# Two transformer layers in one kernel: how the router's choices, rank sums, slot map, compressed keys and last sums are divided among the engines

## What is computed

```
x = h                                        # (4, 256, 256): 1024 tokens of 256
xn = layernorm(x)
x = x + attention0(xn) + moe0(xn)            # moe0: 32 experts, top 6, and 2 shared experts
xn = layernorm(x)
x = x + attention1(xn) + moe1(xn)            # moe1: 8 experts, top 2
```

## Time and profile before

| | us |
|---|---|
| median of 3 runs | 557.43 (556.4 to 557.67) |
| the profiled execution | 554.29 |
| its span in the trace | 552.5 |
| TensorE busy | 511.5 (93%) |
| VectorE busy | 358.2 (65%) |
| ScalarE busy | 312.7 (57%) |
| GpSimd busy | 295.2 (53%) |

### The profile page before, as it was taken

How to read it: one execution, slowest core, us unless ns; L and a number is a source line. 1 busy time by engine, 2 the same in 40 slices (tenths; PEclk the granted TensorE clock), 3 DMA queues, 4 the chain that set the end, 5 groups by cost and what they waited for, 6 DMA issues and landing times.

```text
span 552.5 us, 9828 instructions
## 1 busy us (share of the span) xinstructions
PE 511.5 (93%) x2951; PEld 393.0 (71%) x2951; DVE 358.2 (65%) x1042; ACT 312.7 (57%) x737; POOL 295.2 (53%) x225
## 2 busy tenths in 40 slices
PE   7998999989899999999999999999977989899981
PEld 6556778879678788788788888888755445465561
DVE  6698835728568366566486383433576979997643
ACT  1224266777786676775776765756422358475520
POOL 1002366787678467475676676743130065888860
PEclk9799999999999999999999999999999899999996
DMA  7981457997999767488586697762675022756677
GB/s 241 356 286 41 138 131 162 225 247 191 322 224 274 191 151 175 109 188 182 120 187 147 141 212 153 178 131 30 171 236 183 1 66 58 102 90 99 89 87 229
DMA packets 87395, 90.41 MB, mean 164 GB/s; under 512 B 26768, under 2 KB 75344, under 8 KB 86960
## 3 DMA queue, kind: packets, MB, share of 16 engines
q1 hardware_dynamic: 66720, 61.50, 38.4%
q0 software_dynamic: 19584, 27.24, 28.4%
q10 hardware_dynamic: 1040, 1.05, 0.6%
HBM read 65.32 MB, written 22.60 MB: 159 GB/s over the span
## 4 chain that ended last, share of the span: by engine, by line
PE 63%; DVE 9%; issue 9%; DMA 8%; ACT 6%; POOL 5%; SPq 0%; POOLq 0%; ACTq 0%; DVEq 0%
PE bank L971 12%; PE bank L567 9%; PE bank L980 6%; PE bank L979 6%; DMA expert_sums<-expert_weights,token_of_slot 4%; PE bank L559 4%; PE bank L524 4%; PE bank L492 3%; PE bank L961 3%; POOL tiles L1173 3%; PE bank L576 3%; POOL expert_sums L1180 2%; PE bank L512 2%; PE bank L542 2%; ACT normed L641 2%
## 5 line engine op out<-in xcount | busy, mean ns | idle before, releaser
L941 POOL DMA_INDIRECT expert_sums<-expert_weights,token_of_slot x79 | 128.2, 1623 | 57.3 <-ACT expert_weights L1003 30.6
L933 POOL DMA_INDIRECT expert_weights<-normed_x,token_of_slot x79 | 87.7, 1110 | 110.3 <-DVE token_of_slot L373 49.0
L971 PE MATMUL bank<-expert_weights 128*88 128x128 f32 x632 | 82.6, 273 | 0.4 <-ACT expert_weights L996 0.4
L971 PEld LDWEIGHTS bank<-expert_weights 128*88 128x88 f32 x632 | 72.8, 156 | 1.6 <-issue 1.3
L567 PE MATMUL bank<-out_weights,expert_weights 128*128 128x256 f32 x256 | 59.9, 380 | 2.6 <-DVE residual L830 1.8
L1180 POOL DMA_INDIRECT expert_sums<-expert_weights,token_of_slot x23 | 46.4, 2019 | 13.7 <-issue 5.6
L567 PEld LDWEIGHTS bank<-out_weights,expert_weights 128*128 128x128 f32 x256 | 46.5, 190 | 9.4 <-issue 2.6
L787 DVE SCALAR_TENSOR_TENSOR expert_weights<-bank,blocks_valid 128x64 f32<-128x64 f32 x32 | 7.2, 224 | 63.1 <-ACT expert_weights L655 63.1
L979 PE MATMUL bank<-expert_weights 88*128 88x256 f32 x158 | 47.1, 379 | 0.0
L980 PE MATMUL bank<-expert_weights 89*128 89x256 f32 x158 | 47.1, 379 | 0.0
L1003 ACT ACTIVATE expert_weights<-bank,chosen_bf 128x256 f32<-128x256 f32 x79 | 37.7, 477 | 16.4 <-PE bank L980 16.0
(11 more groups left out here) (283 smaller groups left out, 1071.0 us busy)
## 6 DMA issues: line engine op xcount, KB each, us to landing
expert_weights<-experts_out SPq DMA_DIRECT2D x79, 192.8 KB, 3.5
expert_weights<-experts_in SPq DMA_DIRECT2D x79, 176.0 KB, 3.7
expert_weights<-L_ffn_wi SPq DMA_DIRECT2D x32, 128.0 KB
expert_weights<-w_comp SPq DMA_DIRECT2D x1, 2048.0 KB, 12.1
expert_weights<-fold_g SPq DMA_DIRECT2D x1, 2048.0 KB, 14.5
expert_sums<-zeros SPq DMA_DIRECT2D x2, 1024.0 KB, 13.5
expert_weights<-L_ffn_wo SPq DMA_DIRECT2D x16, 128.0 KB
normed<-expert_sums SPq DMA_DIRECT2D x2, 1024.0 KB, 6.7
```

The source lines that it names most:

```text
L933: nc.gpsimd.indirect_dma_start(xt0[g % 4], None, xn0, bass.IndirectOffsetOnAxis(ap=MAP[:, g:g + 1], axis=0)).then_inc(gathered[g % 4], 16)
L941: nc.gpsimd.indirect_dma_start(sums0[g % 2], bass.IndirectOffsetOnAxis(ap=MAP[:, g:g + 1], axis=0), yt0[g % 4], None, compute_op=ALU.add). ...
L971: ins = nc.tensor.matmul(ps[5][0:DHB, c * P:(c + 1) * P], w[:, k * DH + c * DHB:k * DH + (c + 1) * DHB], xT0[g % NXT][:, k * P:(k + 1) * P ...
```

## The change

Six things are altered. (1) Layer 0's logits come in two banks, 2 and 6, and `lg_ps` is raised after each half; VectorE adds the bias and makes the choices of a half at a time (`choose_dve`). The first `shared_up` moves between the two halves in TensorE's program. (2) The running sum over the tiles is gone from VectorE, in both layers. TensorE makes it: one matmul of all nine groups of columns by the triangular matrix, then eight by the ones, each over all later tiles through a repeated operand. (3) The 79-wide one-hots of the map are made in two steps: GpSimd subtracts (slot tile less column number), and ScalarE squares that and takes relu(token - token * square), which is the token's number where the difference is 0, and 0 elsewhere. VectorE keeps the 128-wide ones. `TOK` has eight more columns, the negated token numbers. (4) The compressed keys of the two halves of the contraction go to rows 0 to 63 and 64 to 127 of bank 2, and VectorE adds the two. (5) The last sums are loaded in quarters, each with a semaphore, and added in quarters. (6) The last `take_project1` goes ahead of these sums.

```
-        TOK = sb("tokens", NT + 1)
+        TOK = sb("tokens", 2 * NT + 1)
...
-        MASKB = sb("chosen_bf16", NT * E0, BF16)
+        MASKB = sb("chosen_bf16", (NT + 1) * E0, BF16)
...
+        def choose_dve(dve, st, E, K, layer, tiles):
             ONEH, PROD, LOGIT, CUM = route_room(layer)
             lg, tp, ti = v3(LOGIT[:, 0:NT * E], NT), v3(TOP[:, :], NT), v3(TOPI[:, :], NT)
-            tf, g3 = v3(TOPF[:, :], NT), v3(GATE[:, 0:NT * K], NT)
+            tf, lo, hi = v3(TOPF[:, :], NT), tiles[0], tiles[-1] + 1
             oh = ONEH[:, 0:NT * K * E].rearrange("p (t k e) -> p t k e", t=NT, k=K)
-            pr = PROD[:, 0:NT * K * E].rearrange("p (t k e) -> p t k e", t=NT, k=K)
-            for t in range(NT):
+            for t in tiles:
                 st(nc.vector.max(tp[:, t, :], lg[:, t, :]))
             st.wait()
-            for t in range(NT):
+            for t in tiles:
                 st(nc.vector.max_index(ti[:, t, :], tp[:, t, :], lg[:, t, :]))
             st.wait()
-            st.link(nc.vector.tensor_copy(TOPF[:, :], TOPI[:, :]))
-            for t in range(NT):
+            st.link(nc.vector.tensor_copy(tf[:, lo:hi, :], ti[:, lo:hi, :]))
+            for t in tiles:
                 st(nc.vector.tensor_tensor(oh[:, t], bc(IOTA[:, 0:E].unsqueeze(1), [P, K, E]),
                                            bc(tf[:, t, 0:K].unsqueeze(2), [P, K, E]), ALU.is_equal))
...
-            st.link(nc.vector.tensor_reduce(v3(CUM[:, 0:NT * E], NT),
-                                            ONEH[:, 0:NT * K * E].rearrange("p (t k e) -> p t e k", t=NT, k=K),
+            st.link(nc.vector.tensor_reduce(v3(CUM[:, 0:NT * E], NT)[:, lo:hi, :],
+                                            ONEH[:, lo * K * E:hi * K * E].rearrange("p (t k e) -> p t e k", t=hi - lo, k=K),
                                             AX, ALU.add))
-            st(nc.vector.tensor_copy(MASKB[:, 0:NT * E], CUM[:, 0:NT * E]))
-            st.link(nc.vector.memset(CUMB[:, 0:E], 0.0))
-            for t in range(1, NT):
-                st.link(nc.vector.tensor_tensor(CUM[:, t * E:(t + 1) * E], CUM[:, (t - 1) * E:t * E],
-                                                CUM[:, t * E:(t + 1) * E], ALU.add))
-            nc.vector.tensor_copy(CUMB[:, E:(NT + 1) * E], CUM[:, 0:NT * E]).then_inc(chosen, 1)
+        def route_dve(dve, st, E, K, layer):
+            CUM, g3, tp = route_room(layer)[3], v3(GATE[:, 0:NT * K], NT), v3(TOP[:, :], NT)
+            st.link(nc.vector.memset(MASKB[:, NT * E:(NT + 1) * E], 0.0))
+            nc.vector.tensor_copy(MASKB[:, 0:NT * E], CUM[:, 0:NT * E]).then_inc(chosen, 1)
...
+        MAPPS, EXPPS, LOGITB = 320, 400, (2, 6)
...
-            st.link(nc.vector.tensor_scalar(MTILE, MTILE, MAGIC, -MAGIC, ALU.add, ALU.add))
+            nc.vector.tensor_scalar(MTILE, MTILE, MAGIC, -MAGIC, ALU.add, ALU.add).then_inc(map_t, 1)
+            dve.wait_ge(map_t, 1)
             st.link(nc.vector.scalar_tensor_tensor(out=v3(MPOS, NT), in0=v3(MTILE, NT), scalar=-float(P), in1=slots, op0=ALU.mult, op1=ALU.add))
         def map_dve(dve, t):
             k = slice(t * K0, (t + 1) * K0)
             if t >= 2:
-                dve.wait_ge(map_c, t - 1)
                 dve.wait_ge(map_ps, t - 1)
-            nc.vector.tensor_tensor(v3(mt[t % 2], K0), bc(IOTA[:, 0:NT0].unsqueeze(1), [P, K0, NT0]),
-                                    bc(MTILE[:, k].unsqueeze(2), [P, K0, NT0]), ALU.is_equal).then_inc(map_b, 1)
             nc.vector.tensor_tensor(v3(ma[t % 2], K0), bc(IOTA[:, :].unsqueeze(1), [P, K0, P]),
                                     bc(MPOS[:, k].unsqueeze(2), [P, K0, P]), ALU.is_equal).then_inc(map_a, 1)
+        def map_pool(pool, t):
+            if t >= 2:
+                pool.wait_ge(map_c, t - 1)
+            nc.gpsimd.tensor_tensor(v3(mt[t % 2], K0), bc(IOTA[:, 0:NT0].unsqueeze(1), [P, K0, NT0]),
+                                    bc(MTILE[:, t * K0:(t + 1) * K0].unsqueeze(2), [P, K0, NT0]), ALU.subtract).then_inc(map_b, 1)
         def map_act(act, t):
             act.wait_ge(map_b, t + 1)
+            nc.scalar.activation(mt[t % 2], mt[t % 2], ACT.Square).then_inc(map_q, 1)
+            act.wait_ge(map_q, t + 1)
             if t >= 2:
                 act.wait_ge(map_ps, t - 1)
-            nc.scalar.activation(mb[t % 2], mt[t % 2], ACT.Copy, scale=TOK[:, t:t + 1]).then_inc(map_c, 1)
+            nc.scalar.activation(mb[t % 2], mt[t % 2], ACT.Relu, scale=TOK[:, NT + 1 + t:NT + 2 + t], bias=TOK[:, t:t + 1]).then_inc(map_c, 1)
...
+            nc.tensor.matmul(bank[:, 0:(NT + 1) * E], BEFOREB[:, :], MASKB[:, 0:(NT + 1) * E], start=True, stop=False)
             for t in range(NT):
-                nc.tensor.matmul(bank[:, t * E:(t + 1) * E], BEFOREB[:, :], MASKB[:, t * E:(t + 1) * E],
-                                 start=True, stop=False)
-                nc.tensor.matmul(bank[:, t * E:(t + 1) * E], ONESB[:, :], CUMB[:, t * E:(t + 1) * E],
-                                 start=False, stop=True)
-            nc.tensor.matmul(bank[:, NT * E:(NT + 1) * E], ONESB[:, :], CUMB[:, NT * E:(NT + 1) * E],
-                             start=True, stop=True).then_inc(rank_ok, 1)
+                later = bank[:, (t + 1) * E:(NT + 1) * E].rearrange("p (n e) -> p n e", e=E)
+                ins = nc.tensor.matmul(later, ONESB[:, :], bc(MASKB[:, t * E:(t + 1) * E].unsqueeze(1), [P, NT - t, E]),
+                                       start=False, stop=(t == NT - 1))
+            ins.then_inc(rank_ok, 1)
...
+            choose_dve(dve, st, E1, K1, 1, range(NT))
             route_dve(dve, st, E1, K1, 1)
...
-            for b in range(B - 1):
+            for b in range(B):
                 take_project1(dve, b)
-            dve.wait_ge(ao_rd, B - 1)
+            dve.wait_ge(ao_rd, B)
             for i in range(2):
                 r = (NT0 + NT1 + i) % 2
-                dve.wait_ge(sum1_ld[r], 16)
-                if i == 0:
-                    st.link(nc.vector.tensor_tensor(X[:, :], X[:, :], SUMS1[r], ALU.add))
-                else:
-                    for b in range(B):
-                        x, y = (z[:, b * TPB * HID:(b + 1) * TPB * HID] for z in (X[:, :], SUMS1[r]))
-                        ins = nc.vector.tensor_tensor(x, x, y, ALU.add)
-                        ins.then_inc(f_ok, 1)
-            dve.wait_ge(f_ok, B)
-            take_project1(dve, B - 1)
+                for b in range(B):
+                    dve.wait_ge(sum1_ld[r][b], 16)
+                    if i:
+                        dve.wait_ge(part_ok, b + 1)
+                    x, y = (z[:, b * TPB * HID:(b + 1) * TPB * HID] for z in (X[:, :], SUMS1[r]))
+                    nc.vector.tensor_tensor(x, x, y, ALU.add).then_inc(f_ok if i else part_ok, 1)
...
-                    sp.dma_start(v3(SUMS1[r], NT), sums1[r][0:T, :].rearrange("(t p) d -> p t d", p=P)).then_inc(sum1_ld[r], 16)
+                    for b in range(B):
+                        sp.dma_start(v3(SUMS1[r], NT)[:, b * TPB:(b + 1) * TPB, :],
+                                     sums1[r][b * S:(b + 1) * S, :].rearrange("(j p) d -> p j d", p=P)).then_inc(sum1_ld[r][b], 16)
                 rows = out.rearrange("b (j p) d -> b p j d", p=P)
                 for b in range(B):
                     sp.wait_ge(f_ok, b + 1)
-                    if b == B - 1:
-                        sp.wait_ge(ao_rd, B)
...
+                pool.wait_ge(ld_c, N_C)
+                pool.wait_ge(map_t, 1)
+                for t in range(NT):
+                    map_pool(pool, t)
                 pool.wait_ge(map_ok, 1)
...
+                st(nc.vector.tensor_scalar(TOK[:, NT + 1:], TOK[:, 0:NT], -1.0, None, ALU.mult))
                 dve.wait_ge(ld_rt, 32)
-                st.link(nc.vector.tensor_tensor(v3(route_room(0)[2], NT), v3(ps[2][:, 0:NT * E0], NT),
-                                                bc(RB[:, :].unsqueeze(1), [P, NT, E0]), ALU.add))
+                for hf in range(2):
+                    lo, hi = hf * NT // 2, (hf + 1) * NT // 2
+                    dve.wait_ge(lg_ps, hf + 1)
+                    st.link(nc.vector.tensor_tensor(v3(route_room(0)[2], NT)[:, lo:hi, :], v3(ps[LOGITB[hf]][:, 0:NT * E0], NT)[:, lo:hi, :],
+                                                    bc(RB[:, :].unsqueeze(1), [P, NT // 2, E0]), ALU.add))
+                    choose_dve(dve, st, E0, K0, 0, range(lo, hi))
                 route_dve(dve, st, E0, K0, 0)
...
-                dve.wait_ge(ck_ps, 1)
+                dve.wait_ge(ck_ps, KC)
                 ckn = CKR[:, 0:D]
-                st.link(nc.vector.tensor_copy(CKR[:, D:], ps[2][0:NB * B, 0:D]))
+                st.link(nc.vector.tensor_copy(CKR[:, 0:D], ps[2][NB * B:2 * NB * B, 0:D]))
+                st.link(nc.vector.tensor_tensor(CKR[:, D:], ps[2][0:NB * B, 0:D], CKR[:, 0:D], ALU.add))
...
-                            ins = nc.tensor.matmul(ps[2][:, t * E0:(t + 1) * E0], xnT3[:, k, t * P:(t + 1) * P],
```

(15 more changed lines are left out.)

25 lines of the change are left out of this document (11 added, 14 removed).

## The result

The changed kernel takes 548.43 us (median of four runs, 546.55 to 551.75) against 556.91 us for the kernel before in the same rounds (555.64 to 557.67). The ratio is 0.986, 95% interval 0.983 to 0.990: 8.5 us less by the medians and 7.6 by the ratio, where 7.9 were forecast and 549.5 us predicted. A repeat gave 0.985.

A forecast was written before the change was run, and what follows sets the result against it. TensorE is busy 93% of the span, but the change touches four stretches where it is not the bound. Terms -5.2 + 3.2 - 1.4 - 2.5 - 2.0 = -7.9 us gave 549.5 us, range 547 to 552 (546.3 to 554.0 with (a), (b), (c)).

The forecast's parts named there:

- choices and ranks, layer 0: Opening: choices in halves, rank sums on TensorE and a clock staying at 1.00 start L304 at 24.9, not 30.07: -5.2 us.
- slot map: Layer 0's map, one-hots partly moved to GpSimd and ScalarE: last `map_pe` 16.3 us after L340, before 13.1: +3.2 us.
- compressed keys: 64 key records in column tiles take 5.0 us, not 7.34; TensorE reaches L1940 at 65.5, not 66.9: -1.4 us.
- middle, 75 to 200 us: Between 75 and 390 us nothing is changed, so a lead won before should pass through: 0.
- layer 1 to its first gather: Layer 1: seven additions and a copy leave VectorE's chain, and TensorE's wait ahead of L1066 shortens: -2.5 us.
- the end: Last sums: VectorE has one quarter left to add after the loads; stores eat part: -2.0 us, between -1.0 and -2.7.
- rival (b): Opening: the clock falls anyway, total -4.6 us, 552.8 us; chance 0.14.
- rival (d): Slot map: GpSimd's subtraction far slower than its memset, deciding from 2.0 us; with 2.5, 561.5 us; chance 0.08.
- rival (a): Slot map: GpSimd and VectorE run freely, map +1.9, total -9.2 us, 548.2 us; chance 0.18.
- the step that charged the map the sum of both engines: Slot map: GpSimd and VectorE block each other, so eight times (1.0 + 0.88) and 0.25 ahead, 15.3 us.
- If the clock holds 2.8, if it falls 1.6: Layer 1: the map ends 2.8 us sooner if TensorE's clock holds, 1.6 if it falls.
- rival (c): Middle full of transfers, or layer 1 gives 1.6 and stores 1.0: about -4.5 us, 552.9 us; chance 0.12.

The follow-up runs named there:

- last quarter late: Changed kernel, but VectorE adds the attention's last quarter behind seven of the eight additions of the expert sums: 547.91 us, ratio 0.983.

## Why the prediction was right, and where it was not

By steps, each against what the traces measured:

| step | forecast | measured |
|---|---|---|
| choices and ranks, layer 0 | -5.2 | -5.1; -6.0 against the second profile of before |
| slot map | +3.2 | +1.8 three times, +2.7 to +3.2 four times |
| compressed keys | -1.4 | -1.4 |
| middle, 75 to 200 us | 0 | +1.6 in nine of twelve executions, 0 in three |
| layer 1 to its first gather | -2.5 | -1.7 to -4.0, -2.9 between the means |
| the end | -2.0 | -0.7 in the mean of seven (-2.2 or +1.4) |
| whole | -7.9 | -8.5 and -8.2 by the medians, -7.6 and -8.6 by the ratios |

**Choices and ranks** came out as worked: the clock held at 1.00, the first half's choices hid in the wait for the second half's logits. The experiments, each taking out one part, divide the term: the halves 1.7 us, the ranks 1.9, and the remaining 1.5 lies ahead of both: the logits end sooner because the clock holds. With the choices whole they still begin at 17.61 us, where before it was 19.18. The clock fell at 14 to 15 us in both profiles of before and held until 26 us in all twelve of changed kernels, which is why rival (b) fell.

**The slot map** came out near its number, but not by the forecast's reason, and that is luck. GpSimd's subtraction takes 0.97 us alone; 1.0 was taken, and rival (d), which needed 2.0, fell. The two engines do hold each other up: no one-hot of VectorE ran in under 1.12 us beside GpSimd where it takes 0.95 alone, so the premise of rival (a) is false. But the step that charged the map the sum of both engines was too dear. Two one-hots took 3.34 us together, 1.67 each beside one subtraction, where the sum of both rows taken alone is 1.93 (1.88 was charged); the blocking is not complete. The Trainium skill, in "SBUF — State Buffer", section "SBUF: two separate sides", has an exclusive lock of the shared port pair for whole instructions, by which a pair could not take less than the sum of the two, 1.93 by these rows; the measured 1.67 decides, so by these rows part of an instruction's span lies outside the lock.

At 1.67 a pair no longer sets the pace alone. Here is the stretch from ScalarE's first Square to its last Relu, first in the run with the end as before, where the clock held, then in the first profile of the changed kernel, where it fell:

```profile
33.52:46.64 13.12, 9.26 (x70) 6.32 (x70) 11.93 (x10) 12.38 (x23) 10.45 (x7) 1.00 0.43 133
```

```profile
33.30:47.52 14.22, 10.74 (x70) 7.56 (x70) 11.09 (x10) 12.41 (x23) 9.42 (x7) 0.88 0.37 115
...
38.62 0.39 ACT L1712 ACTIVATE expert_weights<-bank 128x256 f32<-128x256 f32 x1 [0.88 <-PE bank L1924]
```

ScalarE is busy for 12.4 of 13.1 us: it is the limit, with VectorE and GpSimd close beneath it. In the three executions in which the clock held (choices whole, end as before, last quarter late), the last `map_pe` started 15.0 to 15.1 us after the map's first step, where the prediction worked out 14.9 with ScalarE as the limit and 16.3 with the sum. So the term was +1.8 and not +3.2. Where the clock fell near 35 to 39 us (three executions), ScalarE's take-out of keys and values waited 0.88 to 1.30 us for TensorE, which the forecast had not charged and which made up for the step that was too dear. That ScalarE is the limit is read from the traces; no run changed its work alone. From the map's first step to its end were 13.9 us in all seven kernels with the one-hots on VectorE (before among them), 15.7 in three of seven on GpSimd, and 16.7 to 17.1 in four. The fourth of these is the one with running sums: its clock held in the map but fell just ahead of it (26.5 to 29.9 us), so that ScalarE was held up by the shared experts' relu and began its first Square 3.15 us after the map's first step in place of 1.66.

**Layer 1** showed the clearest quantity of the study. From the copy of the chosen (L283) to the first gather pass, in fourteen executions, only these: 20.30, 21.27 and 21.36 us with running sums (before twice, and the experiment), and with the ranks on TensorE 17.33 or 17.34 six times and 18.64 or 18.65 five times. The 1.66 us of VectorE's additions is in all; the rest is the clock. The chain of the repeat shows the dear case, columns as in the earlier trace rows:

```profile
423.54 5.40 PE bank L1070 x8
428.94 1.87 PE bank L1093 x8
```

In the first profile the same eight records took 3.70 us at a clock of 1.00, VectorE was the limit, and the chain came to

```profile
440.43 0.04 issue
440.48 1.93 PE bank L1093 x7
```

without an idle gap on VectorE. "If the clock holds 2.8, if it falls 1.6" was right both ways; what the prediction didn't see is that the same program does the one or the other from run to run.

**The step that failed** is the sentence that between 75 and 390 us nothing is changed and a lead passes through. From the first to the thirty-third scatter of layer 0 pass 124.05 to 124.63 us in five executions (before twice, the repeat, and two with the map on VectorE) and 125.08 to 128.92, 126.1 in the mean, in nine. The nine are exactly those in which the scatter of the ninth tile held GpSimd for 3.25 to 3.69 us instead of 1.6. The traces show the cause. In the nine the scatter started 0.05 to 0.50 us after the start of VectorE's L782 and ended 1.46 us after its end, every time; in the five it started 0.02 to 1.00 us ahead of L782 and took 1.58. From the ninth scatter to the tenth pass 4.8 to 5.3 us in the nine and 3.5 to 4.5 in the five. It is the blocking that the prediction had read from the earlier trace rows and charged to the map alone: it did not ask where else a scatter stands this close to a VectorE instruction with two inputs in SBUF, and in the profile of before 0.02 us decided it.

The scatter of the twenty-eighth tile was caught by the same instruction in four executions (2.99 to 3.55 us, again ending 1.46 behind it); in two of these the distance to the thirty-third stayed at 124.6, so there it cost nothing. The loss is one that rival (c) allowed for, 1.6 us against the 3.4 by which (c) lies above the forecast, though (c) gave full transfers as the reason; it is nearly all of the lead in one execution. A lead isn't lost everywhere in the middle: from 200 us on, the distance between any two executions stays the same but for single tiles that come back to it (188.2 us from the thirty-third scatter to the last of layer 0 in all fourteen). No run moved the scatter and L782 apart on purpose, and what decides which of the two comes first I did not follow up; that before was spared in two of two and the changed kernels were caught in nine of twelve may be chance.

**The end** has its price right for one of two cases. The prediction let only the last additions count and did not ask which of two chains, scatter and load, or heads, transposition and projection, is the last on VectorE. The change puts the attention's last quarter ahead of the eight additions, and where that quarter came late (541.24 above) it carries 4.9 us with it. Part of the lateness is TensorE's clock, which fell during the last projection in two of the three.

**The sum.** Added up for the two profiles of the changed kernel against the two of before, in means: -3.1 at the first scatter, +1.2 to the thirty-third, -2.8 in layer 1, -0.2 at the end, -4.9 in all, and the spans differ by 4.65. The runs without a profile differ by more, since the profiled ones of the changed kernel lie 2.3 us above the mean of its ten spans (546.5), and those of before 1.2 us below the mean of 53 (554.6). What the spans alone can tell of the remainder is the clock: its mean over the span was 0.981 before and 0.992 after, and among the 53 executions of before, 0.010 more clock went with 3.9 us less span (correlation -0.72). By that line the clock accounts for 4.5 of the 8.1 us; the prediction had 4.2 (3.3 in the opening, 0.9 in layer 1). This is a correlation and not a test. The total fell into place partly by luck: a loss in the middle and a poorer end were made up, as far as the correlation tells, by clock that before had lost more often, or for longer, than its one profile showed; and in the map, where the clock fell, too dear a pair and a clock that was taken to hold cancelled each other.

## What to carry to other kernels

Where a part of VectorE's work goes to GpSimd, set the time that each takes beside the other against the time won: here 0.64 us left VectorE, and 0.4 came back on each of its own instructions, with two steps of ScalarE in place of one, which left ScalarE hardly any slack. Where a scatter is issued on GpSimd near a long VectorE instruction with both inputs in SBUF, look at which starts first: 0.05 us on the wrong side made it 3.69 us in place of 1.58. When an addition that must wait for a slow transfer is put ahead of others in an in-order queue, ask which is later in the bad execution, not in the one that was profiled; the late quarter costs 0.9 us in the good executions, and the bad ones were 3.6 us behind those. And before a lead of a few microseconds is credited through a stretch full of transfers, look at two or three profiles of the same kernel: single executions differed here by more than most of the terms.
